# Where the second layer's weights are split, where three biases are added, and which products stand ahead of the last transposes

## The reference

```python
xq = layer_norm(x, qn_w, qn_b); ctx = layer_norm(context, cn_w, cn_b)
q = xq @ q_w; k, v = split(ctx @ kv_w)
attn = softmax(where(mask, -max, q @ k.T * scale))
x = x + (attn @ v) @ proj_w + proj_b
h = layer_norm(x, n2_w, n2_b)
out = x + gelu(h @ fc1_w + fc1_b) @ fc2_w + fc2_b     # hidden size 2048
```

## Time and profile before

| | |
|---|---|
| median of 3 runs | 1055.22 us (1054.14 to 1057.02) |
| the profiled execution | 1055.71 us, its span 1053.8 us |
| PE busy | 1032.3 us, 98% of the span |
| DVE, ACT, POOL busy | 834.3, 434.1, 357.5 us (79%, 41%, 34%) |
| attention | 0 to 381 us |
| first block, sets 1 to 7 | 385 to 540 us |
| last three blocks | 540 to 1054 us |

### The profile page before, as it was taken

One profiled execution on the slowest core, in us unless ns is written; L12 is line 12 of the kernel. 1 busy time (PEld: TensorE's weight loads), 2 busy tenths in 40 slices (PEclk: granted clock), 3 DMA queues, 4 the chain that ended last, 5 costly groups with the idle time before them and its releaser, 6 DMA issues.

```text
span 1053.8 us, 16336 instructions
## 1 busy us (share of the span) xinstructions
PE 1032.3 (98%) x5857; PEld 854.9 (81%) x5857; DVE 834.3 (79%) x1323; ACT 434.1 (41%) x766; POOL 357.5 (34%) x259
## 2 busy tenths in 40 slices
PE   8999999999999999999999999999999999999998
PEld 6787888888888777778778888887888888888887
DVE  8889999999998899898886667687766677666655
ACT  5343344453444565544442334342433353222221
POOL 3555566666788744233504000303100210300000
PEclk9999999999999999999999999999999999999999
DMA  7012122221210185445577535336535343834312
GB/s 265 9 45 71 51 72 81 74 62 61 93 51 21 50 318 190 163 178 193 187 269 280 208 129 183 149 132 204 232 129 215 134 149 132 317 115 175 119 71 81
DMA packets 52279, 149.19 MB, mean 142 GB/s; under 512 B 10801, under 2 KB 19033, under 8 KB 44019
## 3 DMA queue, kind: packets, MB, share of 16 engines
q1 hardware_dynamic: 51627, 147.25, 38.9%
q10 hardware_dynamic: 584, 1.06, 0.3%
HBM read 108.13 MB, written 39.85 MB: 140 GB/s over the span
## 4 chain that ended last, share of the span: by engine, by line
PE 81%; DVE 10%; issue 4%; DMA 3%; POOL 2%; ACT 0%; DVEq 0%; SPq 0%; POOLq 0%; ACTq 0%
PE bank L1792 29%; PE bank L1762 25%; PE bank L1638 7%; PE bank L1594 7%; PE bank L1575 4%; PE bank L1626 3%; PE bank L1607 2%; PE bank L1771 1%; DMA xr<-in_x 1%; PE bank L1585 1%; DVE gT L1391 1%; DMA x_scratch<-xr 1%; DVE acc L1399 1%; DVE hop L1361 1%; DVE hring L1375 1%
## 5 line engine op out<-in xcount | busy, mean ns | idle before, releaser
L1792 PE MATMUL bank<-w2r,gT 128*128 128x512 f32 x1536 | 360.3, 391 | 3.6 <-DVE acc L1399 3.4
L1792 PEld LDWEIGHTS bank<-w2r,gT 128*128 128x128 f32 x1536 | 286.5, 188 | 66.3 <-DVE acc L1399 7.4
L1762 PE MATMUL bank<-hop,w1r 128*128 128x512 f32 x1344 | 312.2, 390 | 1.3 <-POOL w2r L776 1.3
L1762 PEld LDWEIGHTS bank<-hop,w1r 128*128 128x128 f32 x1344 | 251.2, 188 | 54.3 <-issue 2.1
L1399 DVE TENSOR_TENSOR acc<-bank,acc 128x512 f32<-128x512 f32 x256 | 176.3, 690 | 102.4 <-PE bank L1792 97.7
L1386 DVE TENSOR_TENSOR ybuf<-bank,ybuf 128x512 f32<-128x512 f32 x224 | 148.3, 688 | 72.5 <-PE bank L1762 68.1
L1036 ACT ACTIVATE ybuf<-ybuf,cols 128x512 f32<-128x512 f32 x128 | 91.6, 716 | 163.0 <-DVE ybuf L1386 163.0
L1391 DVE TENSOR_TENSOR gT<-ybuf,gT 128x512 fp32r<-128x512 f32 x128 | 102.6, 822 | 0.0
L676 POOL TENSOR_TENSOR S<-S,rsum 128x1232 f32<-128x1232 f32 x32 | 75.3, 2352 | 61.6 <-DVE rsum L1190 61.6
L641 POOL TENSOR_TENSOR hrs<-hve,mhalf 128x1 f32<-128x1 f32 x32 | 18.0, 561 | 220.6 <-DVE hve L1371 220.6
L784 POOL TENSOR_TENSOR acc<-acc,fc2b 128x512 f32<-128x512 f32 x32 | 42.1, 1330 | 122.1 <-DMA acc<-x_scratch 122.0
(11 more groups left out here) (111 smaller groups left out, 1429.6 us busy)
## 6 DMA issues: line engine op xcount, KB each, us to landing
w1r<-w_scratch SPq DMA_DIRECT2D x24, 1792.0 KB, 7.2
w2r<-w_scratch SPq DMA_DIRECT2D x24, 1024.0 KB, 5.3
w_scratch<-w1r SPq DMA_DIRECT2D x8, 1792.0 KB, 6.3
xr<-in_x SPq DMA_DIRECT2D x16, 512.0 KB, 4.1
x_scratch<-xr SPq DMA_DIRECT2D x16, 512.0 KB, 2.8
hring<-x_scratch SPq DMA_DIRECT2D x32, 256.0 KB, 3.1
acc<-x_scratch SPq DMA_DIRECT2D x32, 256.0 KB, 4.1
w_scratch<-w2r SPq DMA_DIRECT2D x8, 1024.0 KB, 9.3
```

The lines of the kernel that those rows point to most:

```text
L1762: mm = pe.matmul(bank_[:, :], w1r[:, w1_slot(s), c, w, kk * P:(kk + 1) * P], hop[i][:, d, kk, :], start=(kk == 0 and n == 0), stop=(kk == ...
L1792: mm = pe.matmul(bY[t % 2][:, :], gT[s % 2][:, j, d, t * P:(t + 1) * P], w2r[:, s % 2, j, w, :], start=(n == 0), stop=(n == 5))
```

## The change

Four edits. (1) ACT's `w2_hi(s)` moves from behind the four gelus of set s to behind the first (sets 1 to 6), and to the head of set 7. POOL's `w2_lo(s)` moves in sets 1 to 5 from the set's end to behind its first `h_rstd`. SP's `store_w2(s)` and `load_w2raw(s + 1)` are issued in set s; before, `store_w2(s - 1)` and `load_w2raw(s)` were. (2) `acc_bias` of tiles 5 to 7 moves from set 1 into the last attention step, and `load_w2raw(0)` on SP behind the loads of these tiles. (3) DVE's `hop_lo(0, 0)` moves within the step of unit 14, past four `masked`, one `maximum`, to just ahead of `av_lo(0)`. (4) PE makes M2 of set 0 ahead of the last unit's `prob_T(0)` and no longer behind it.

```diff
@@ sync_program
         p_projb.wait(sp, last_unit, UT - 1)
         load_acc(0, BT - 3)
-        load_w2raw(0)
         sp.wait_ge(d_x2st, 16 * (NU - 1))
         load_acc(0, BT - 2)
         load_acc(0, BT - 1)
+        load_w2raw(0)
         load_w2raw(1)
...
                 if first:
-                    if s > 0:
-                        store_w2(s - 1)
-                    if s > 1:
-                        load_w2raw(s)
                     if 0 < s < SETS - 2:
                         load_w1raw(s + 2)
+                    store_w2(s)
+                    if 0 < s < SETS - 1:
+                        load_w2raw(s + 1)
...
                     if first:
-                        store_w2(s)
@@ gpsimd_program
             if tail == 2:
                 w1_sums(1)
+                for t in range(BT - 3, BT):
+                    acc_bias(0, t)
...
                         h_rstd(b + 1, t)
-                        if first and s == 1 and n == 0:
-                            for i in range(BT - 3, BT):
-                                acc_bias(b, i)
-                if first and s > 0:
+                        if first and n == 0:
+                            w2_lo(s)
+                if first and s > 0 and s not in TILES:
                     w2_lo(s)
@@ scalar_program
+                if first and s == SETS - 1:
+                    w2_hi(s)
                 if first and s == 0:
                     t_proj.wait(act, last_unit, UT - 1)
                 else:
                     m1_copy(b, s)
...
                     gelu(b, s, 0)
+                if first and 0 < s < SETS - 1:
+                    w2_hi(s)
...
                 gelu(b, s, 3)
-                if first and s > 0:
-                    w2_hi(s)
@@ vector_program
-            if tail == 1:
-                hop_lo(0, 0)
             if scores:
                 masked(0, 2)
                 masked(0, 3)
...
             if tail == 1:
+                hop_lo(0, 0)
                 av_lo(0)
@@ tensor_program
             if tail == 2:
                 mul(0, 0, M1, first=True)
+                mul(0, 0, M2, first=True)
             if back:
                 prob_T(0)
-            if tail == 2:
-                mul(0, 0, M2, first=True)
```

## The result

The changed kernel took 1053.61 us, the median of 20 runs (1050.58 to 1056.61). The kernel before took 1056.25 us on the same chip in the same comparison (20 runs, 1053.55 to 1061.32). The ratio is 0.9976, with a 95% interval of 0.9966 to 0.9986: 2.5 us less, between 1.5 and 3.6. The forecast was 3.6 us less and 1051.6 us. The change is a gain, but within the 0.3% that the prediction had set as its border. The profiled execution took 1052.38 us, with a span of 1050.6 us against 1053.8 before: 3.2 us less.

What follows compares the result with a forecast made beforehand. PE, busy in 98% of the span, was read as the bound, its gaps as the gain. Terms -3.55 + 0.35 - 0.4 = -3.6 us gave 1052.1 on the profiled execution, 1051.6 for the median; 8-in-10 range 1049.3 to 1053.7.

Steps and rivals of the forecast that it cites:

- Edit 1, sets 2 to 5: Second-layer stretches of sets 2 to 5: fall to block 1's lengths with w2_lo early, 3.55 us won (3.0 to 3.7).
- Set 6: Set 6: no edit counts; w2_lo waits in both kernels for POOL's hop_T and sums, starting at 512.54.
- Edit 3, `hop_lo(0, 0)`: Unit 14's step: hop_lo(0, 0) stands behind less_max(0), delaying maximum(1) and the last av_lo(0); loss 0.5 us.
- Edit 4, M2: Last attention step: M2 fills PE's 1.56 us wait, but av_lo(0) sets what follows; 0, range 0 to -1.0 us.
- Edit 2, the biases: Last attention step: biases and DVE's work exclude each other, set 0's joins 1.0 us late (0 to 1.7).
- Set 1: Third tile at 400.05, then 9.0 us to set 2 at 409.05; net loss 0.35 us (-1.2 to +1.0).
- Set 7: Set 7: end wait of 1.3 us won, about 0.9 lost in the third tile behind late m1_copy; net 0.4 won.
- The first: Rival: biases hide in DVE's idle time and in waits, set 2 begins 1.0 us earlier; 1050.6 us, chance 18%.
- the second: Rival: both transition edits pay, hop_lo(0, 0) not held, M2 fills the gap, biases hidden; 1049.1 us, chance 10%.
- the third: Rival: sets 2 to 5's excess came from first-layer w1_lo and w1_sums; half the 3.55 stays, 1053.4 us, chance 20%.
- The fourth: Rival: set 7's raw load lands 10.7 us after request, m1_copy at 527.6; 6.2 us more, 1057.8 us, chance 5%.
- The fifth: Rival: early w2_hi waits for late raw weights in every set, each set loses; about 1058 us, chance 2%.

Runs made afterwards that it cites:

- only1: Changed kernel with only the early w2_hi and w2_lo kept; hop_lo(0, 0) and M2 moved back, biases in set 1 behind w2_lo(1); ratio to before 0.996.
- split2: Kernel before with each w2_lo made as two instructions of 512 elements instead of one of 1024; ratio to before 0.9972.
- again: The changed kernel, word for word, measured a second time; ratio to the kernel before 0.9968.
- late7b: Changed kernel with w2_hi(7) behind the fourth gelu of set 7, the early request of its raw weights kept; ratio to the kernel before 0.9948.
- u_bias: Changed kernel with the three biases back in set 1, behind w2_lo(1); ratio to the kernel before 0.9971.
- u_m2: Changed kernel with M2 of set 0 behind the last prob_T(0) again; ratio to the kernel before 0.9994.
- u_hop: Changed kernel with hop_lo(0, 0) back between the first two and second two masked of unit 14's step; ratio to the kernel before 0.9969.
- mid: Changed kernel with hop_lo(0, 0) between the second pair of masked and maximum(0); ratio to the kernel before 0.9942.
- best2: Changed kernel with hop_lo(0, 0) ahead of maximum(0), w2_hi(7) behind the fourth gelu, biases spread from w2_lo(0) through set 1; 1049.02 us, ratio to before 0.9916.
- late7: Changed kernel with w2_hi(7) behind the fourth hop_hi of set 7, ahead of its second gelu; ratio to the kernel before 0.998.

## Why the prediction was right in its mechanism, and which steps failed

The mechanism held: a DVE and a POOL instruction that exclude each other for a whole instruction, and what each edit makes or parts of such pairs. Three steps failed. In set 7 the term for the third tile was 0.9 us and measured 1.83, so that the set lost 0.28 us where 0.4 were to be won. Set 6 was put at nothing and gave 0.52 us. And the 3.6 us worked out on one trace were taken off a median of three runs, 1055.22 us, as if the runs had to show all of them: the trace did give 3.45, but the runs of the comparison gave 2.5, and from 1056.25. The first two misses nearly cancel, which is luck. The third is the larger part of the distance to the measured time, and why the runs gained less stays open.

**Edit 1, sets 2 to 5: right.** Forecast -3.55 us, measured 84.50 - 88.06 = -3.56, stretch by stretch at the lengths of block 1. `only1` gives the same gain without the other edits, and `split2` shows by another way that the lock on `w2_lo` was the cause.

**Set 6: missed, 0.5 us.** The prediction said that no edit counts there, since `w2_lo(6)` waits for POOL's sums in both kernels. It took 21.05 us instead of 21.57. The step that failed is "starts at 512.54", taken as a fixed time when it was the end of a chain. In the kernel before, DVE and POOL at the turn from set 5 to set 6 and in set 6:

```profile
493.61 2.39 POOL L776 TENSOR_TENSOR w2r<-w2raw,w2r 128x1024 fp32r<-128x1024 f32 x1
...
498.61 2.59 POOL L764 TENSOR_TENSOR T<-raw 128x1024 f32<-128x1024 f32 x1 [2.62 <-ACT raw L1004]
...
493.82 2.46 DVE L1375 TENSOR_SCALAR hring<-hring,hmv,hrs 128x512 f32<-128x512 f32 x1
...
498.27 3.48 DVE L1391 TENSOR_TENSOR gT<-ybuf,gT 128x512 fp32r<-128x512 f32 x2
...
514.00 1.81 DVE L1356 TENSOR_TENSOR w1r<-w1raw,w1r 128x512 fp32r<-128x512 f32 x2
```

`w2_lo(5)` held `h_normed` (2.46 us), so the last two `g_lo` of set 5 ran late enough to meet POOL's `hop_T` (3.48 us for two), which itself took 2.59 us and then, at 501.17, 2.85 where it is worth 2.40. In the changed kernel those `g_lo` end before `hop_T` begins, and all four `hop_T` take 2.40 to 2.42. `w2_lo(6)` then starts 14.82 us into the set instead of 15.79, and the two `w1_lo(7)` that it used to hold take 1.30 us instead of 1.81. PE's wait fell from 0.73 to 0.21 us. This is read from the two traces, and sets 2 to 6 of `again` show it once more; no run tested it alone.

**Edit 3, `hop_lo(0, 0)`: right.** Forecast +0.5, measured +0.65 by undoing it, and the row came as 2.72 us, as told. By the Trainium skill ("SBUF — State Buffer", on the port shared by DVE and GpSimd) whichever instruction begins first keeps the pair for its whole length. The trace agrees: `less_max(0)` ended at 354.73, and 355.81 less that is 1.08 us, about the 1.2 that `hop_lo` takes alone.

**Edit 4, M2: right, nothing.** -0.01 us by the trace. The row expected at 373.4 came at 373.77 with a wait of 0.69 us; the rest of the expected wait stood at `av(0)`, for ACT's copies of the transposes (0.83 us), as the prediction had said of M2's cover. (Its opening calls the 1.3 us for `w2_lo` one of PE's two longest waits; the 1.56 us that this edit was to fill was longer.) The wait of 1.27 us at 356.47, for the first `av_lo` of the step, wasn't foretold. It is the same delay of `hop_lo(0, 0)`, met one product group earlier by a PE that had come early.

**Edit 2, the biases: right mechanism, size 0.73 instead of 1.0.** The idle time of DVE absorbed some more, 0.31 us ahead of a `y_add`.

**Set 1: right.** Forecast +0.35 us at set 2's start; measured 61.97 - 61.62 = +0.35. The parts were +1.5 and 9.0 to the next set in the forecast, and +1.36 and 9.13 in the trace. That the sum came to the hundredth is luck: 0.14 us too little in one part and 0.13 too much in the other.

**Set 7: mis-sized, +0.28 us instead of -0.4.** The end wait went, 1.32 us for the forecast's 1.3. The term for the third tile was 0.9 us and should have been 1.83. The prediction counted from the end of `w2_lo(6)`, 3.4 us ahead of the set's first product, and put the landing 5.5 us behind it. That end came as told (511.46, 3.37 us ahead), but SP first issued the store and began the load's request at 511.85, 2.98 us ahead of the product; from there the landing took 5.9 us. By the prediction's own count the load took 6.3 us, past the 6 that it had named as a sign of failing. Together these put `m1_copy` 3.86 us behind that product, not 3.1, and PE lost these 0.76 us and a little more, 0.93 over the 0.9 forecast. Of the 0.51 that this wait costs beyond the 1.32, some 0.2 came back in gaps too small to be listed, hence +0.28 and not more. `late7b` shows the rest: with `m1_copy` at 1.56 and `w2_lo(7)` out of DVE's way the set takes 20.76 us.

**The sum.** -3.56 in sets 2 to 5, +0.35 before them, -0.52 in set 6 and +0.28 in set 7 are the -3.45 of the trace, against -3.6 forecast. Two misses of opposite sign nearly cancelled. In the span 0.24 of that went back, since this execution reached the step later, in code that the change does not touch. The runs show less: -2.5 us in the first comparison (1.5 to 3.6), -3.4 in the second (1.9 to 4.9). The forecast size is at the edge of the first and inside the second.

**The level.** The median of before was 1055.22 us of three runs and is 1056.25 of twenty, 1.0 us more; four comparisons gave 1054.96 to 1057.61. That carries over to the 1051.6, and it is half of the distance of 2.0 us to 1053.61; the other half is the smaller gain. The forecast also stood 0.45 us beyond its own border of 0.3%, so the choice between "faster" and "the same" hung on less than the runs can tell.

**The rivals.** The first (biases hide) fell to the 3.21 us row and `u_bias`; the second to `u_m2` and `u_hop`; the third to the stretches of sets 2 to 5. The fourth named the right place, `m1_copy` behind a DMA, but its landing of 10.7 us did not come. Its size also holds a slip: 10.7 less the 5.5 taken is 5.2 us, not 6.2, which makes that rival 1056.8 and not 1057.8. The fifth did not occur: in sets 1 to 6 of the changed kernel ACT never waits for raw weights.

**Still open** is why the runs of the changed kernel gain less than its trace in the first comparison. The clock that fell behind the 1.83 us gap in one of two traces could be a part of it, but the other kernels do not bear that out. In the comparison of `late7b`, `mid`, `best2` and `split2` the runs gain as much as the traces or more (5.5, 6.1, 8.9 and 3.0 us against 5.2, 4.8, 7.2 and 2.95), although `mid` has the gap too; in that of `u_hop`, `u_m2`, `u_bias` and `late7` they gain less (3.3, 0.6, 3.1 and 2.1 against 4.1, 3.4, 3.9 and 4.0), although the gap of `late7` is only 1.31 us. The difference goes with the comparison more than with the gap. Each of these gains is uncertain by 1 to 3 us.

## What to carry to other kernels

An instruction on one engine that shares a lock with another engine should be priced by what it meets, not by its own time: list what both engines run in the new place, and look for a stretch in which the other reads PSUM, or put it ahead of the instruction that sets the other engine off. Where no such place is free, split the long instruction; that alone was worth 2.95 us here by the trace, and 3.0 (1.5 to 4.5) by the runs. A wait for a DMA belongs behind everything on its engine that doesn't need it, and a delay removed in one loop round should be followed into the next rounds, where it removes or makes other meetings.

## What the runs showed of the hardware that I had not expected

- **A gap of under 2 us can cost twice.** Behind a wait of 1.83 us in `again`, TensorE's granted clock fell to 0.50 and 0.74 in the four microseconds from 529, which cost 1.62 us. In `split2`, behind the 1.90 us at the block's end, a stretch of 5 us had a granted clock of 0.66, and the next set took 22.2 us where that set takes 20.4 to 20.5 in the other kernels. Stretch behind the wait in `split2`:

```profile
540.00:545.00 5.00, 5.00 (x17) 3.92 (x16) 4.36 (x5) 0.63 (x2) 0.00 (x0) 0.66 0.66 228
```

  Waits of 1.8 us in the traces of six kernels (the changed one, `u_hop`, `u_m2`, `u_bias`, `only1`, `mid`) had no such drop, so it comes in some executions and not in others.
- **DVE and POOL take turns.** With three biases on POOL and three instructions on DVE the work lasted 5.24 us for 3.78 and 4.9 for 2.2. One by one, the biases took 1.30, 2.29 and 1.74 us (1.26 alone) and the DVE instructions 1.73, 1.78 and 1.51. Each outlasts the end of the other engine's instruction before it by about its own length alone: the first bias ends at 378.16, `hop_lo(0, 5)` at 379.25, the second bias at 380.40, a `w1_lo` at 380.95, the third bias at 382.10, the other `w1_lo` at 382.38.
- **Two DMA requests took 1.40 us to issue** on SP right behind that of a 1 MB store (511.85), where a single one takes 0.33. The second of the two starts at 512.3, 0.45 us behind the first, and `w2_hi(7)` needs both. How much of the late landing that makes isn't shown.
